# Attention scores on TensorE: float32r parts in 32-row tiles, and each max-side pair followed by an exp-side pair

## What is computed

```
scores = jnp.einsum('bhqd,bhkd->bhqk', q, k) * scale
scores = scores.at[:, :, 0, -1].set(NEG)      # attention a only, and its mirror
weights = jax.nn.softmax(scores, axis=-1)
out = jnp.einsum('bhqk,bhkd->bhqd', weights, v)
...
x = x + attn_a(_layernorm(x))
x = x + ffn(_layernorm(x))
x = x + attn_b(_layernorm(x))
x = x + ffn(_layernorm(x))
```

## Time and profile before

| | us |
|---|---|
| median of 3 runs (990.22 to 991.79) | 991.68 |
| span of the profiled execution, first to last instruction | 987.4 |
| median of the runs over that span | 4.3 |
| TensorE busy in the span | 917.8 (93%) |
| VectorE busy | 787.2 (80%) |
| ScalarE busy | 772.6 (78%) |
| GpSimd busy | 666.2 (67%) |

### The profile page before, as it was taken

How to read it: one execution, slowest core, us unless ns; L and a number is a source line. 1 busy time by engine, 2 the same in 40 slices (tenths; PEclk the granted TensorE clock), 3 DMA queues, 4 the chain that set the end, 5 groups by cost and what they waited for, 6 DMA issues and landing times.

```text
span 987.4 us, 27821 instructions
## 1 busy us (share of the span) xinstructions
PE 917.8 (93%) x10286; PEld 513.9 (52%) x10286; DVE 787.2 (80%) x1394; ACT 772.6 (78%) x1299; POOL 666.2 (67%) x1280
## 2 busy tenths in 40 slices
PE   2589999999999999999999999999999998999885
PEld 1345555545555555555655555555555555654544
DVE  1688888898888888888788887888788878778524
ACT  2168888888888888888888888888888877887863
POOL 8465666667775886768676786768687585764442
PEclk9899999999999999999999999999999999999987
DMA  6577555444444443444444343444444454344001
GB/s 183 150 219 204 154 149 168 141 152 142 135 140 121 150 134 120 145 121 146 119 138 149 121 143 119 153 119 128 136 136 142 125 153 123 118 137 135 5 22 43
DMA packets 144694, 131.66 MB, mean 133 GB/s; under 512 B 9616, under 2 KB 127536, under 8 KB 144432
## 3 DMA queue, kind: packets, MB, share of 16 engines
q1 hardware_dynamic: 143456, 128.49, 43.8%
q10 hardware_dynamic: 1104, 1.41, 0.5%
HBM read 73.76 MB, written 55.57 MB: 131 GB/s over the span
## 4 chain that ended last, share of the span: by engine, by line
PE 67%; ACT 10%; DVE 9%; POOL 5%; issue 4%; DMA 3%; SPq 1%; POOLq 1%; ACTq 1%; DVEq 0%
PE values_bank L774 21%; PE ring L789 11%; PE ring L803 10%; PE m_bank L898 6%; DVE nmax L598 5%; PE m_bank L910 4%; PE m_bank L959 3%; PE m_bank L943 3%; PE m_bank L920 3%; ACT probs L669 2%; PE m_bank L931 2%; ACT hT L722 2%; ACT L713 2%; DMA k_stack<-scratch 2%; DMA scratch<-parts 1%
## 5 line engine op out<-in xcount | busy, mean ns | idle before, releaser
L598 DVE TENSOR_REDUCE nmax<-ring 128x4 f32<-128x1024 f32 x512 | 605.1, 1219 | 98.0 <-PE ring L789 97.0
L669 ACT ACTIVATE probs<-ring 128x1024 f32<-128x1024 f32 x512 | 518.2, 1025 | 54.8 <-PE ring L803 50.4
L774 PE MATMUL values_bank<-probs,values 128*32 128x256 f32 x4096 | 274.9, 386 | 0.7 <-ACT probs L669 0.6
L789 PE MATMUL ring<-k_stack,q_stack 64*128 64x256 bf16 x2048 | 201.2, 277 | 22.7 <-DMA k_stack<-scratch 18.6
L489 POOL TENSOR_SCALAR xy<-x,mv,rstd 128x128 f32<-128x128 f32 x256 | 200.6, 793 | 7.9
L803 PE MATMUL ring<-q_stack,k_stack 64*128 64x256 bf16 x2048 | 189.4, 273 | 8.5 <-DVE nmax L598 7.2
L774 PEld LDWEIGHTS values_bank<-probs,values 128*32 128x32 f32 x4096 | 107.1, 109 | 89.8 <-issue 37.2
L413 POOL TENSOR_SCALAR mparts<-nmax 128x32 bf16<-128x32 f32 x64 | 13.9, 217 | 188.0 <-DVE nmax L598 187.8
L789 PEld LDWEIGHTS ring<-k_stack,q_stack 64*128 64x128 bf16 x2048 | 70.3, 95 | 132.0 <-issue 56.0
L803 PEld LDWEIGHTS ring<-q_stack,k_stack 64*128 64x128 bf16 x2048 | 78.0, 94 | 93.9 <-issue 52.0
L511 POOL TENSOR_TENSOR parts<-rest,parts 128x512 bf16<-128x512 f32 x64 | 74.1, 1158 | 5.4
(11 more groups left out here) (102 smaller groups left out, 1084.0 us busy)
## 6 DMA issues: line engine op xcount, KB each, us to landing
q_stack<-scratch SPq DMA_DIRECT2D x128, 256.0 KB
k_stack<-scratch SPq DMA_DIRECT2D x128, 256.0 KB
scratch<-parts SPq DMA_DIRECT2D x128, 192.0 KB, 2.2
scratch<-parts SPq DMA_DIRECT2D x128, 128.0 KB, 2.2
scratch<-parts SPq DMA_DIRECT2D x128, 64.0 KB, 2.4
out<-x SPq DMA_DIRECT2D x16, 256.0 KB, 2.7
x<-in_x SPq DMA_DIRECT2D x3, 768.0 KB, 7.3
q_stack<-maxT SPq DMA_DIRECT2D x128, 12.0 KB
```

The lines of the kernel that those rows point to most:

```text
L598: nc.vector.tensor_reduce(dst, src, axis=AX.X, op=ALU.max, negate=True).then_inc(max_done, 1)
L669: nc.scalar.activation(probs[g % 2][:, c:c + 2, :, :], pair_of("exps", n, p)[:, :, :].rearrange("p x (k q) -> p x k q", k=TILES), ACT.Exp) ...
L774: last = nc.tensor.matmul(values_bank[32 * c:32 * (c + 1), a * TOKENS:(a + 1) * TOKENS], values[turn % RING][:, k, PER_GROUP * g + c, :], ...
L789: last = nc.tensor.matmul(pair_of("scores", turn, p)[:, a, t * TOKENS:(t + 1) * TOKENS], q_stack[z][rows, p, t * P:(t + 1) * P], k_stack[z ...
```

## The change

1. q and k are split into two parts instead of three. The high part is written as float32r, the other is the remainder, and the matmuls read both as float32r. Three slots of 8 rows instead of six, and 8 rows for mask and maximum: 32 rows for a head instead of 64, in a stack of the same bytes. A pair lies on two of four row groups, and the max-side and the exp-side pair of one part p lie on different ones.
2. On TensorE each max-side pair is directly followed by the exp-side pair of the same p.
3. The last weighting group of the turn before moves from p=1 to p=0, `down` moves from behind the max-side pair of p=4 to behind the weighting group of p=3, and the ring's place for `up` moves behind part 5.
4. On ScalarE the copy of the summed values comes at p=0 ahead of that of the maxima, and the copies of maxima, QK, v, attention output and x come one part later.
5. GpSimd drops two of four operations of the split of the maxima and two of four of that of q and k; the transposes of the maxima become float32; SP issues 8 transfers a turn instead of 12.

```diff
-Q_PARTS = (0, 0, 0, 1, 1, 2)
-K_PARTS = (0, 1, 2, 0, 1, 0)
+Q_PARTS = (0, 0, 1)
+K_PARTS = (0, 1, 0)
-BLOCK = 64
+BLOCK = 32
+ROW_GROUPS = P // BLOCK
+QUADS = HEADS // ROW_GROUPS
+HALF_PAIRS = PAIRS // 2
+def max_place(m):
+    return m // HALF_PAIRS, m % HALF_PAIRS
+def exp_place(p):
+    return 1 - p // HALF_PAIRS, p % HALF_PAIRS
...
-        DOWN_AFTER, UP_AFTER = 3, 4
+        DOWN_AFTER, UP_AFTER = 3, 5
...
                         if p == 5:
                             pool.wait_ge(hi_ready, (n + 4) + 1)
-                            nc.gpsimd.tensor_tensor(rest[i][:, :, :], qk32[i][:, :, :], parts[i][:, 0], ALU.subtract).then_inc(rest_done, 1)
-                        if p == 6:
...
+                            nc.gpsimd.tensor_tensor(parts[i][:, 1], qk32[i][:, :, :], parts[i][:, 0], ALU.subtract).then_inc(parts_ready, 1)
...
                             last = nc.tensor.matmul(pair_of("scores", turn, p)[:, a, t * TOKENS:(t + 1) * TOKENS],
-                                                    q_stack[z][rows, p, t * P:(t + 1) * P], k_stack[z][rows, p, :],
+                                                    q_stack[z][rows, j, t * P:(t + 1) * P].bitcast(FP32R), k_stack[z][rows, j, :].bitcast(FP32R),
                                                     start=(t == 0), stop=(t == TILES - 1))
...
                     if live(n + 2):
                         max_side(n + 2, p)
-                    if live(n) and p == 0:
-                        exp_side(n, 0)
+                    if live(n):
+                        exp_side(n, p)
+                    if p == 0 and live(n - 1):
+                        weigh(n - 1, 3)
...
-                    if p == 1 and live(n - 1):
-                        weigh(n - 1, 3)
...
-                    if p == 4 and group_at(n) is not None:
+                    if p == 3 and group_at(n) is not None:
                         down(group_at(n))
```

More of the change, by code:

```diff
@@ L8 @@
 BF16 = mybir.dt.bfloat16
+FP32R = mybir.dt.float32r
 U32 = mybir.dt.uint32
@@ L368, in step @@
                         if live(n + 2):
[L369 to L376, removed]
-                            sp.dma_start(D[at:at + count].rearrange("s p t -> p s t"), k_src).then_inc(bounced[i], 16)
+                            sp.wait_ge(stack_in[(n + 2) % 2], (n + 2) // 2 * 32 + 32)
+                        high = [parts[i][:, 0, qk].unsqueeze(1).broadcast_to([P, 2, TOKENS]) for qk in range(2)]
+                        sp.wait_ge(hi_ready, (n + 4) + 1)
+                        sp.dma_start(D[0][:, 0:2], high[0]).then_inc(bounced[i], 16)
+                        sp.dma_start(D[1][:, 0:3:2], high[1]).then_inc(bounced[i], 16)
+                        sp.wait_ge(parts_ready, (n + 4) + 1)
+                        sp.dma_start(D[0][:, 2], parts[i][:, 1, 0]).then_inc(bounced[i], 16)
+                        sp.dma_start(D[1][:, 1], parts[i][:, 1, 1]).then_inc(bounced[i], 16)
                     if 2 <= n + 3 < len(CHUNKS):
@@ L675, in step @@
                             act.wait_ge(max_in[(n - 1) % 2], (n - 1) // 2 * 32 + 32)
-                        nc.scalar.copy(maxT[(n + 1) % 2][:, :],
-                                       m_bank[:, :].bitcast(BF16)[0:6 * PAIRS, 0:TOKENS]).then_inc(maxT_ready, 1)
-                    if p == 0 and batch_at(n, 2) is not None:
+                        nc.scalar.copy(maxT[(n + 1) % 2][:, :].rearrange("h (t p) -> h t p", t=TILES),
+                                       m_bank[0:2 * HEADS, :].rearrange("h (w p) -> h w p", p=P)[:, 0::3]).then_inc(maxT_ready, 1)
+                    if p == 1 and batch_at(n, 2) is not None:
                         b = batch_at(n, 2)
@@ L685, in step @@
                         nc.scalar.copy(hotT[:, :, :].rearrange("p a b -> p (a b)"), m_bank[0:TOP * EXPERTS, WIDTH + ITEMS:WIDTH + 5 * ITEMS]).then_inc(weight_ready, 1)
-                    if p == 0 and batch_at(n, 3) is not None:
+                    if p == 1 and batch_at(n, 3) is not None:
                         b = batch_at(n, 3)
```

141 lines of the change are left out of this document (53 added, 88 removed).

## The result

The changed kernel takes 1122.5 us (median, 1117.3 to 1127.9) against 991.0 for the kernel before in the same session: 1.133 times as long, 95% interval 1.129 to 1.137. So 131.5 us were added where 90 were forecast. Its profiled execution spans 1115.4 us. In it TensorE is busy less of the time than before (89% against 93%) and VectorE, which has hardly more work, stands in more than twice the share of the chain of work that ended last.

The account below looks back on a forecast made before the run. TensorE was taken to set the turn (busy 12.80 of 12.83 us). Turns 71, bursts 18, routing 4, less 3 at the start, gave 90 us on a median of 991.7: 1082 us, range 1035 to 1175.

Parts of the forecast that it names:

- the turn: One step of the program, some 60 with this work: 14.01 us against 12.83, 1.18 more each, 71 us.
- the way through VectorE: Time between successive exp-side score pairs set by max reduction and hand-over: 1.59 us, or 1.15 if VectorE was behind.
- A pair's scores are done 0.39 after its start: Score matmuls on TensorE: results complete 0.39 us after a pair starts, VectorE's reduction starting 0.05 later.
- M(p) started 0.11 before E(p): On TensorE the max-side score pair of part p starts 0.11 us before the exp-side pair of that part.
- the price of no overlap: Rival: max-side and exp-side score pairs don't run side by side; 0.1 us a turn, 1085 us; chance 5%.
- One pass: Float32r score matmuls stream once: a round of 0.11 us, with a median record near 270 ns.
- the two-pass rival: Float32r score matmuls take two passes, a round of 0.22 us: 2.79 us more a turn, 1170 us; chance 20%.
- The saving that was a rival: Reductions run ahead of TensorE, whose lighter work sets the turn at 11.75 us: 927 us; chance 10%.
- Bursts: Steps with expert work, 13 of them: 5.4 us above a turn against 4.06, up matmuls waiting; 18 us.
- Routing: VectorE's small routing work, now on a way without slack: 4 us added, from 0 to 12.
- The start: Filling of the first stacks, with split steps dropped and lighter rounding: 3 us gained, from 0 to 10.
- At nothing: Changes priced at zero: GpSimd's other dropped operations, fewer SP transfers, the moved copy of oT, the dropped bf16 identity.

Follow-up runs that it names:

- the order alone: Kernel before with its three bf16 parts and 64-row tiles, but the changed kernel's TensorE and ScalarE order: 1088.4 us, ratio 1.099.
- the pair with half of the reduction: Max reduction over half of the keys only, in the changed kernel (1043.7 us, ratio 1.054) and in the kernel before (977.2 us, 0.986).
- two bf16 parts: Changed kernel, same order and 32-row tiles, with its two parts in bf16 instead of float32r: 1079 to 1097 us, ratio 1.092.
- the third order: Changed kernel's float32r tiles, with max-side pairs up to one ahead of exp-side pairs on TensorE: 1001.0 us, ratio 1.011 to the kernel before.

## Why the prediction was right, and where it was off

**The sign and the mechanism held.** E(p) right behind M(p) waits for the reduction of M(p-1), the idle time alternates, and the turn grows though there is less to compute: shown by the order alone (97 us) and by the pair with half of the reduction. The waits stand where I put them: E(5) 0.24 and E(7) 0.29 in the timelines above, E(1) and E(2) each 0.05 behind the end of the reduction that frees their buffer (648.83 and 650.21, their wait hidden under the max-side pair ahead of them), and VectorE idle 0.15, 0.51, 0.39 and 0.59 ahead of M(1), M(3), M(4) and M(6). TensorE's busy share of the turn is 94%, not 84%: the records are longer (a first matmul 380 ns) than the distance they cost.

**The term that was mis-sized is the turn, 1.18 forecast and 1.85 measured**; over 60 turns this is 40 of the 41.5 us that were missing. By parts, from the start of E(p) to that of E(p+1):

| | p=0 | 1 | 2 | 3 | 4 | 5 | 6 | 7 | sum |
|---|---|---|---|---|---|---|---|---|---|
| forecast | 1.68 | 1.36 | 1.67 | 2.24 | 1.59 | 1.80 | 1.59 | 2.08 | 14.01 |
| after | 1.88 | 1.38 | 1.56 | 2.33 | 1.81 | 1.81 | 1.81 | 2.09 | 14.67 |
| two bf16 parts | 1.77 | 1.27 | 1.55 | 2.33 | 1.70 | 1.71 | 1.70 | 1.98 | 14.02 |

Three parts miss by 0.2: 0, 4 and 6. At p=4 and p=6 the way through VectorE is the longer one, as forecast, and two steps of it failed. "A pair's scores are done 0.39 after its start": 0.50, since each float32r load takes 184 ns. "M(p) started 0.11 before E(p)": 0.013, since E's first round does not queue behind M's but runs with it. The bf16 kernel has the second error alone and shows 1.70, after has both and shows 1.81. At p=0 E(0), which runs with M(0), started 0.66 after WO instead of 0.76, and E(1) 2.54 after WO instead of 2.44 (2.43 in the bf16 kernel).

The sum of the bf16 row agrees with the forecast by luck: its parts 1, 2, 5 and 7 are each 0.1 shorter than forecast, which makes up for the others. One of these is a reading that was wrong. QK's 1.16 in the earlier trace rows holds 0.10 of waiting: what follows QK there is M(3), at 506.01, 0.05 after the end of the exponential of E(1) that frees its buffer (504.93 + 1.03). In after QK costs 1.06. (A slip besides: the price of no overlap, by its own 0.1 a turn, is 1088 us and not 1085.)

**Round and run.** One pass was right, and the two-pass rival fell: 275 ns for a second-round matmul, and a lone pair 0.11 dearer than in bf16 where two passes in both rounds would add 0.22. The sign that I had named for it, the median of the score matmuls, misled: in line 794 it is 379 ns, which was to mean two passes, because half of its records are first rounds. The Trainium skill ("FP8 and Floating Point Precision", TensorE Precision Notes) has four passes for true FP32, and reduced FP32 cut to a shorter format on reading; that the latter is a single pass is shown by the records here. But a round is 0.22 all the same, the upper bound that I had named and not taken, and I put that down to the load. A run of M and E still costs about what I said, 0.45 against 0.43: two rounds of 0.22 instead of three of 0.11 and 0.10. A lone pair costs 0.43 instead of 0.32. I took the matmul's records for the whole price. The row for the load was there in the trace of before, and I had not looked at it; a load of 128 columns of float32 weights in the v projection:

```profile
L920 PEld LDWEIGHTS m_bank<-wa,xnT x128: 186/192/338, 17.5 to 440.2; 128*128 128x128 f32 x128
```

**The saving that was a rival** exists where nothing waits: the two bf16 parts in the order of before have it. The Trainium skill's rule that tiling speeds up TensorE but not the emptying of PSUM ("TensorEngine Tiling (Array Packing)", PSUM Bottleneck) agrees with the traces: in that kernel M and E take 0.34 together instead of 0.55, and a reduction takes 1.22 us on average there as in the kernel before.

**Bursts.** An undisturbed one is 19.85 - 14.67 = 5.18 over a turn, against 5.4 forecast; `up` waits 1.02 for the exponential instead of 1.35. Yet the ten bursts ahead of the late steps lost 38.1 us, 1.87 each of it the turn, so 1.9 each beyond it, where an undisturbed one lost 1.1 (16.89 to 19.85, less the turn). Two things fill the gap: in three of them the clock fell, as the last section shows, and the five that hold routing work as well lost more, the three of them at a whole clock 0.65 each (20.99 against 17.37 in the kernel before, for one).

**Routing** was forecast at 4 us (0 to 12). The 13 steps with routing and no expert work lost 22.7 us, 1.75 each, no more than a quiet turn; its price lies in the five bursts above, some 3 us at 0.65 each. **The start** gained 5.8, within the bounds; that this is the lighter split isn't shown. The float32r tiles in the order of before drop the same operations and gained 0.4, with weighting groups at 1.86 instead of 1.00 us from 50 to 73 us, where its profile shows a granted clock of 1.00 all the same. **At nothing** was wrong for GpSimd in one place: the float32r tiles and the two bf16 parts, each in the order of before, gain 3 and 9 us in the late steps, the former though its turns are longer. There the chain of the kernel before runs through the split, whose second half, with the subtraction of line 511, the change drops (start us, duration us, what):

```profile
797.61 1.17 POOL rest L505
799.57 1.16 POOL parts L511
```

That this is what the late steps gain is read from the chain and was not run by itself. In after it lies under the loss of the turn.

## What to carry to other kernels

Before interchanging two users of one small ring, write down for each buffer who empties it and how far ahead of the next fill he is. Here an order that put a filler directly behind the one that his emptier had yet to work on made the two engines wait for each other in alternation, with bf16 as with float32r matmuls. Price a matmul by the distance between the starts of two rounds and not by its record, loads included, and follow a new order through the rare heavy steps too: they took back nearly all that the third order gained.

## What the hardware showed that I had not expected

**Four row groups start as one.** Pairs on rows 0 to 63 and 64 to 127 start 13 ns apart and share both rounds (rows of part 4 above), though they are issued one after the other; in the kernel before, with 64-row tiles, the second pair starts 0.23 us behind the first (512.54 and 512.77).

**A float32r matmul streams like bf16 and loads like float32**: 275 against 268 ns for a second-round matmul, 184 against 93 a load.

**A wait of 1 us was sometimes followed by half the clock.** Two bursts of after, one with the clock whole, and the one at 402 to 424, which took 21.71 instead of 19.85. Timelines of TensorE, and for the second the windows of 2 us with the columns of the earlier trace rows:

```profile
544.24 0.39 PE L821 MATMUL ring<-biasu_parts,pick 96*128 96x256 bf16 x2 [1.01 <-ACT probs L658]
544.47 1.06 PE L829 MATMUL ring<-wu,hT 128*128 128x128 f32 x8
...
546.78 1.07 PE L763 MATMUL values_bank<-probs,values 128*32 128x256 f32 x16
```

```profile
409.14 0.39 PE L821 MATMUL ring<-biasu_parts,pick 96*128 96x256 bf16 x2 [1.02 <-ACT probs L658]
409.37 1.21 PE L829 MATMUL ring<-wu,hT 128*128 128x128 f32 x8
...
410.81 1.91 PE L829 MATMUL ring<-wu,hT 128*128 128x128 f32 x8
...
413.08 1.28 PE L763 MATMUL values_bank<-probs,values 128*32 128x256 f32 x16
```

```profile
408.00:410.00 2.00, 0.98 (x12) 0.85 (x9) 1.10 (x3) 1.99 (x5) 0.00 (x0) 1.00 0.00 0
410.00:412.00 2.00, 2.00 (x12) 1.87 (x12) 0.69 (x1) 0.34 (x1) 0.00 (x0) 0.53 0.00 0
412.00:414.00 2.00, 2.00 (x22) 1.21 (x20) 0.98 (x5) 0.47 (x1) 0.00 (x0) 0.61 0.00 0
414.00:416.00 2.00, 1.82 (x24) 1.03 (x16) 1.17 (x2) 1.05 (x2) 0.00 (x0) 1.00 0.00 0
```

In both, TensorE waited 0.24 for E(5) and then about 1.0 for `up`. In the second the granted clock is 0.53 and 0.61 in the 4 us behind it, so mostly its lower level, 1.2 GHz; eight `up` matmuls take 1.91 instead of 1.06, and the step 1.86 more (it lies in attention a, whose quiet turn is 0.25 longer at a whole clock). Waits of one length were followed by both, so what decides between them stays open. None of the 13 bursts of the kernel before lost its clock, but neither did those of the three bf16 parts in the order of after, which wait up to 1.2 us ahead of `up`: the wait alone does not do it. No sum of mine contained this price.
